# A Mamba and mixture-of-experts block on one core: front products re-spaced between the scans, and constant products added to TensorE

## The reference

```python
h = layernorm(x) * gamma + beta
u, z = split(h @ in_proj.T)                      # 256 channels each
uc = silu(causal_conv4(u) + conv_b)
dt, Bm, Cm = split(uc @ x_proj.T)                # 64, 16, 16
delta = softplus(dt @ dt_proj.T + dt_b)          # 256 channels
state = exp(delta * A) * state + delta * Bm * uc # 256 x 16 states, over 2048 steps
y = (sum_n(state * Cm) + uc * D) * silu(z)
x = layernorm(x + (y @ out_proj.T + x))
probs, experts = top_k(softmax(x @ Wg + bg), 2)  # 8 experts, 128 -> 512 -> 128, gelu
x = layernorm(x + sum_k(probs_k * expert_k(x)))
```

## Time and profile before

| | us |
|---|---|
| three timed runs | 889.17, 895.06, 895.17 |
| median | 895.06 |
| profiled execution, its own time | 891.96 |
| its span | 890.2 |
| first scan to last scan (eight units) | 56.3 to 639.9 |
| mean granted clock of TensorE | 0.764 |

### The profile page before, as it was taken

One profiled execution on the slowest core, in us unless ns is written; L12 is line 12 of the kernel. 1 busy time (PEld: TensorE's weight loads), 2 busy tenths in 40 slices (PEclk: granted clock), 3 DMA queues, 4 the chain that ended last, 5 costly groups with the idle time before them and its releaser, 6 DMA issues. The chain is left out here.

```text
span 890.2 us, 12242 instructions
## 1 busy us (share of the span) xinstructions
PE 678.5 (76%) x2905; PEld 311.1 (35%) x2905; DVE 687.3 (77%) x1350; ACT 423.3 (48%) x884; POOL 530.7 (60%) x526
## 2 busy tenths in 40 slices
PE   3768989878778988878888976878631998899920
PEld 2322222222222322222232221212221888888820
DVE  2167788989998897899889899999732677777754
ACT  3537458357465534735655453324110555455424
POOL 5124546745687757677676677867863455455433
PEclk9885867877987776787797666556555899999975
DMA  3074455565376855547465465655003666666646
GB/s 82 0 202 106 95 127 133 121 152 131 82 189 172 196 135 134 122 115 172 105 142 124 112 142 118 161 120 123 24 27 91 166 177 170 176 168 178 181 128 175
DMA packets 60390, 117.37 MB, mean 132 GB/s; under 512 B 8817, under 2 KB 37297, under 8 KB 52257
## 3 DMA queue, kind: packets, MB, share of 16 engines
q1 hardware_dynamic: 56000, 107.60, 49.4%
q0 software_dynamic: 4320, 8.99, 3.1%
HBM read 100.21 MB, written 16.35 MB: 131 GB/s over the span
## 5 line engine op out<-in xcount | busy, mean ns | idle before, releaser
L532 POOL TENSOR_TENSOR hc<-hs,Crep 128x1024 f32<-128x1024 f32 x128 | 300.1, 2355 | 188.2 <-PE bank L759 102.0
L1295 DVE TENSOR_TENSOR_SCAN hs<-bank,state,flow 128x512 f32<-128x512 f32 x256 | 314.6, 1268 | 58.5 <-ACT bank L1061 53.2
L1061 ACT ACTIVATE bank<-bank,negA 128x512 f32<-128x512 f32 x256 | 165.1, 662 | 253.4 <-PE bank L749 242.0
L749 PE MATMUL bank<-delta,sel 32*128 32x512 f32 x512 | 195.0, 839 | 83.3 <-DVE hs L1295 83.2
L1285 DVE TENSOR_TENSOR flow<-flow,bank 128x2048 f32<-128x2048 f32 x63 | 142.7, 2265 | 0.0
L749 PEld LDWEIGHTS bank<-delta,sel 32*128 32x128 f32 x512 | 50.8, 237 | 212.8 <-DVE hs L1295 145.4
L1189 ACT ACTIVATE flow<-bank,b1T 128x128 f32<-128x128 f32 x284 | 81.1, 369 | 79.8 <-PE bank L926 77.6
L759 PE MATMUL bank<-hc,kc 128*32 128x512 f32 x512 | 91.2, 795 | 6.1 <-POOL hc L532 6.1
L698 PE MATMUL bank<-hT,wtapT 128*128 128x512 f32 x128 | 88.9, 822 | 6.9 <-issue 4.9
L926 PE MATMUL bank<-flow 128*128 128x128 f32 x568 | 83.0, 291 | 14.0 <-issue 9.1
L641 POOL DMA_INDIRECT results<-flow,idn x71 | 69.9, 984 | 33.2 <-issue 31.4
(11 more groups left out here) (180 smaller groups left out, 774.8 us busy)
## 6 DMA issues: line engine op xcount, KB each, us to landing
flow<-du_d SPq DMA_DIRECT2D x63, 1024.0 KB, 7.1
flow<-L_ffn_W SPq DMA_DIRECT2D x71, 256.0 KB
xg<-xs SPq DMA_DIRECT2D x71, 66.0 KB
hs<-results SPq DMA_DIRECT2D x16, 256.0 KB, 4.8
du_d<-du SPq DMA_DIRECT2D x28, 128.0 KB, 3.1
xin<-L_attn_x SPq DMA_DIRECT2D x8, 256.0 KB, 3.1
out<-hc SPq DMA_DIRECT2D x8, 256.0 KB, 2.5
results<-flow,idn POOLq DMA_INDIRECT x71
```

The lines of the kernel that those rows point to most:

```text
L532: nc.gpsimd.tensor_tensor(hc[:, Q % 2, two, :], hs[:, Q % 2, two, :], Crep[u % 3][:].unsqueeze(1).broadcast_to([P, 2, T]), ALU.mult).then_ ...
L749: ins = nc.tensor.matmul(dbank[i][:], sel[32 * i:32 * i + 32, q % 4, :], delta[u % 2][32 * i:32 * i + 32, q // 4, :])
L1061: nc.scalar.activation(dbank[G % 4][:], dbank[G % 4][:], ACT.Exp, scale=negA[:, ch:ch + 1]).then_inc(s_ex, 1)
L1295: nc.vector.tensor_tensor_scan(hs[:, Q % 2, j, :], dbank[G % 4][:], flow[Q % 3][:, j, :], state[:, Q // QUADS % 2, Q % QUADS, j:j + 1], AL ...
```

## The change

TensorE's front work moves by up to two intervals, `spread_b` from g 29 to g 31 behind everything else of the unit; ScalarE's evacuations move with it. In units 1 to 5, at ten places in the order, `keep_busy` adds products of two constant tiles of ones (bf16, 512 columns, 44 a unit) into the front bank that comes next, after a wait until that bank has been drained. GpSimd sets the new tile `idle_rhs` once. Results are not changed: the next user of the bank overwrites it.

```diff
+KEPT_BUSY = {3: (5, "c", 1), 7: (4, "u0", 2), 11: (2, "u0", 2), 13: (2, "u0", 2), 15: (2, "out", -1), 19: (6, "u1", 2),
+             21: (4, "z0", 2), 23: (8, "z1", 2), 25: (5, "xn", -1), 27: (6, "logits", -1)}
...
+            link(nc.gpsimd.memset(idle_rhs[:], 1.0))
...
+            def keep_busy(newest, times):
+                drained(pe, newest - 1)
+                for _ in range(times):
+                    nc.tensor.matmul(fbank[(newest + 1) % 2][:], ones[:], idle_rhs[:])
...
-                    if g == 29 and late:
-                        spread_b(j + 1)
...
                     if late:
+                        if g == 0:
+                            proj_dt(j + 1, 0)
                         if g == 1:
-                            proj_dt(j + 1, 0)
+                            proj_dt(j + 1, 1)
                         if g == 2:
-                            proj_dt(j + 1, 1)
-                        if g == 4:
                             spread_c(j + 1)
...
+                    if late and g == 31:
+                        spread_b(j + 1)
+                    if early and g in KEPT_BUSY:
+                        times, what, ahead = KEPT_BUSY[g]
+                        keep_busy(fill_of(j + ahead, what), times)
```

More of the change, by code:

```diff
@@ L104, in mamba_moe @@
         ones = sb("ones", [P, P], BF16)
+        idle_rhs = sb("idle_rhs", [P, T], BF16)
         w2_sb = sb("w2_sb", [P, E, HK, D])
@@ L817, in host @@
                         first_host(g)
+                        if g == 31:
+                            spread_b(1)
                         continue
                     if late:
+                        if g == 0:
+                            proj_dt(j + 1, 0)
                         if g == 1:
-                            proj_dt(j + 1, 0)
+                            proj_dt(j + 1, 1)
                         if g == 2:
-                            proj_dt(j + 1, 1)
-                        if g == 4:
                             spread_c(j + 1)
-                    if g == 5 and j >= 2:
+                    if g == 4 and j >= 2:
                         ranks(j - 2)
                     if early:
-                        if g == 6:
+                        if g == 5:
                             xhat_T(j + 2)
-                        if g in (8, 9, 10, 12):
-                            conv_u(j + 2, 0, ((8, 9, 10, 12).index(g),))
+                        if g in (7, 8, 10, 11):
+                            conv_u(j + 2, 0, ((7, 8, 10, 11).index(g),))
                     if g == 13:
@@ L836, in host @@
                         out_proj(j - 1, (0, 1))
-                    if g == 16:
+                    if g == 15:
                         out_proj(j - 1, (2, 3))
                     if early:
-                        if g in (17, 18, 20, 21):
-                            conv_u(j + 2, 1, ((17, 18, 20, 21).index(g),))
+                        if g == 16:
+                            conv_u(j + 2, 1, (0,))
+                        if g == 18:
+                            conv_u(j + 2, 1, (1,))
+                        if g == 19:
+                            conv_u(j + 2, 1, (2, 3))
+                        if g == 20:
+                            proj_z(j + 2, 0)
                         if g == 22:
-                            proj_z(j + 2, 0)
-                        if g == 24:
                             proj_z(j + 2, 1)
-                    if g == 25:
+                    if g == 24:
                         xn_T(j - 1)
-                    if g == 28:
+                    if g == 27:
                         logits(j - 1)
@@ L1103, in host @@
                         if g == 4:
+                            c_evac(j + 1)
                             exponential(j + 1)
@@ L1106, in host @@
                             one_plus(j + 1)
-                        if g == 6:
-                            c_evac(j + 1)
                         if g == 8:
@@ L1113, in host @@
                             xhats(j + 2)
-                        if g == 6:
+                        if g == 5:
                             h_evac(j + 2)
-                        if g == 13:
+                        if g == 12:
                             u_evac(j + 2, 0)
+                        if g == 20:
+                            u_evac(j + 2, 1)
                         if g == 21:
-                            u_evac(j + 2, 1)
-                        if g == 22:
                             z_evac(j + 2, 0)
-                        if g == 24:
+                        if g == 23:
                             z_evac(j + 2, 1)
```

## The result

The changed kernel is slower: 906.99 us median of four runs (900.9 to 909.78) against 893.64 (889.17 to 895.17) on the same chip, a ratio of 1.0146 [1.0104, 1.0187] (in brackets, here and below, the 95% interval). Of all the runs of this document two, both of "Tap 0 back", were in a slower state; its median holds them, its ratio doesn't. Its profiled execution took 909.78 us, 17.8 more than that of before (891.96), and its span is 908.0 us. The loop over the units took 598.9 us (57.2 to 656.1) in place of 583.6 (56.3 to 639.9), so 15.3 of the 17.8 us arose there.

The account below looks back on a forecast made before the run. VectorE was taken as the bound, with 53.2 us of scans' waits for ScalarE's exponential as the whole prize; 9.9 us from units 1 to 5 plus 4.5 from units 0 and 6, off 891.96, gave 877.5 us (range 860 to 896).

Parts of the forecast that it names:

- Part 4: Start of units 1 to 5, summed: stalls of 4.3 + 0.4 + 0.7 = 5.4 us left in each, 9.9 us won.
- P: Start of pair 4, counted from scan 0's start: 4.35 us fast, 7.2 us if the clock falls before `spread_c`.
- rival B: Slower, chance 0.12: clock falls at g 2, doesn't recover on fills; 16.9 us lost, 4.5 won, 904.4 us.
- Part 1: Unit's end: `spread_b` to g 31 saves 3.17 us in unit 3, 4.5 us in units 0 and 6 together.
- Part 2: Front work an interval earlier: `spread_c` starts 1.0 us after scan 0 starts, `add_states` done at 3.1.
- Part 3: Price of a fill: 0.25 us fast, 0.45 slow; only the five at g 3 on the path, 1.25 or 2.25.
- Part 4's first half: Unit's start up to scan 6: pair 4 at 7.2 us, a stall of 4.3 us before scans 4 to 6.
- The clock: One fall per unit in place of three, none at softplus or Silu; units 1 to 5 at about 0.85.
- rival C: No change, chance 0.14: fills at g 4 to g 9 eat `spread_b`'s gain; 891.4 us (884 to 899).
- the two things named as what would make the forecast wrong: GpSimd late with hc, so scans wait for L532; or ScalarE's early evacuations waiting for TensorE; no size given.

Follow-up runs that it names:

- Tap 0 back: The changed kernel with the first convolution tap of each unit put back from g 7 to g 8: 891.27 us, ratio 0.9919.
- One-hots early: The changed kernel with the next unit's one-hots moved from behind scan 0 to behind scan 30 of the unit before: 926.46 us, ratio 1.0335.
- GpSimd waits for the one-hots: "Tap 0 back" with GpSimd's last product by C in units 1 to 6 held until the one-hots are done: 881.02 us, ratio 0.9896.
- the best layout: The kernel before with `spread_b` at g 31 ahead of `add_states`, GpSimd's wait for the one-hots and `logits` at g 27, no fills: 864.22 us, ratio 0.9658.
- Only `spread_b`: The kernel before with `spread_b` alone moved from g 29 to g 31, behind `proj_x` and `add_states`: 892.07 us, ratio 0.9938.

## Why the prediction was wrong, point by point

**The step that failed** is in Part 4: "Tap 0 waits for hT, four fills and pair 8 follow", with 0.4 us before scan 9. Tap 0 at g 7 takes the front bank that the ranks filled, and so waits for the run update behind scan 6 too. The change's order on TensorE shows the wait, a second semaphore beside that of ScalarE (line L702):

```
L702 MATMUL bank<-hT,wtapT 128x512 [waits front_bank_drained_by_act,front_bank_drained_by_dve]
```

VectorE frees the bank at 304.42 in unit 3, when scan 6 is done; hT had been there since 302.27. The tap ran at the slow level (2.07 us) with the fills behind it (1.91), so the pair of g 8 came 6.5 us after its release. Forecast for scans 8 and 9 were 2.0 us in five units; the trace shows 24.4 (0.4 of it in unit 6). Moving the tap back gives 1.0146 → 0.9919, and the tap alone costs 1.27% in the kernel before. Both directions were run, so it is shown that the tap's place ahead of the pair made the loss.

The wait is only a part of what came late there. By the forecast's own terms the pair of g 8 starts at P + 8.15 (12.5 in rival B's account, at P = 4.35). With P = 7.8 it started at P + 11.8, 3.7 us later. The tap itself started at P + 8.1, 2.2 us behind hT, which had been forecast as what it waits for (without the run update it would still have stood behind `add_states` until 302.87, 1.6 us earlier than it started). The rest is the level: tap and fills took 3.7 us, where about 2.1 had been counted. So Part 4 also had it wrong that the clock, once back, stays: it came back for 3.4 us and fell again ahead of the tap. In units 2 to 5 the tap started within 0.1 us of the run update's end; unit 1 has no ranks, and there it waited for hT. No run separates the wait from the slow tap and fills.

**A term that was missing**: VectorE's own operations. I priced the one-hots at 0.4 us of VectorE's time, as they were, and never asked what GpSimd does beside them once the scans before them stop waiting. VectorE was busy 9.3 us longer in the loop: one-hots 9.4 us more, the addition of the softplus parts (L1258, median 1966 ns, before 1197) 4.3 more, and others less. It can't simply be added to the waits: in units 3 to 5 it stands in place of the wait for the late pair of g 4. With the tap back its cure gave nothing that could be told; that it is no second cause of the loss in the changed kernel itself is argued from there, since the one run on that kernel ("One-hots early") only moved the collision. In the kernel with `spread_b` at g 31 alone it decides 1.3%.

**Part 1** was right about the place and too hopeful about the price. 19.9 us before scan 30 went to none. But "`add_states` and a product fit" holds only while the scans wait; in the run of `spread_b` alone the inflows waited 8.6 us for it. Ahead of `add_states`, with GpSimd held back and `logits` an interval earlier, it brings 3.4%. The waits of units 0 and 6 fell by 3.5 us of the 4.5, but unit 6 itself didn't become shorter (70.1 us for 69.8): its one-hots collided too, and VectorE was busy 1.1 us longer.

**Part 2** held: `spread_c` waited for the Relu of dt0 and started at +1.7 (+1.0 forecast), `add_states` and the fills behind it.

**Part 3** held in the price: at the slow level the five fills of g 3 take 2.31 us in the timeline above; at the fast level the five of g 25 take

```profile
346.07 1.24 PE L799 MATMUL bank<-idle_rhs,ones 128*128 128x512 bf16 x5
```

A single record lasts 0.38 us (`376/379/379` for the least, median and longest of those fills) and overlaps the next, so start to start is (1.24 - 0.38) / 4 = 0.215 us, and twice that at the slow level; 0.25 and 0.45 had been taken. The Trainium skill ("TensorE: Matmul & The Clock Gate", section "Back-to-back issue gap") gives by its formula for the warm clock 0.216 us for 512 columns, and 0.131 us as what a sustained stream reaches. The trace agrees with the first and not with the second. What failed is "they hide where VectorE's interval is long". Three pairs of kernels say they don't: 1.0146 and 1.0039, 0.9919 and 0.9848, 0.9779 and 0.9658. The one with fills is slower by 0.7 to 1.2% each time; of the second pair the intervals just touch. Nor do "only the five at g 3" lie on the path: the four at g 7, which Part 4 itself sets ahead of the pair of g 8, took 1.9 us there.

**Part 4's first half** held: P = 7.8 us in unit 3 (7.2), and with the collision out of the way scans 4, 5 and 6 wait 2.23 + 0.73 + 1.13 = 4.1 us in unit 3 of the experiment (4.3 forecast). Scan 27 kept 0.7 in four units and 1.1 in unit 5.

**The clock** went as forecast at the softplus work and at Silu. One fall became two: it rose on the five fills at 296.80, fell at 300.20, ahead of the tap, and came back at 317.30. The mean of units 1 to 5 (0.86, 0.82, 0.83, 0.84, 0.91) is the 0.85 named.

**Rival B** had the sign, and with 904.4 us nearly the time, by a road that is half right. Its slow tap (1.9 us) and four slow fills (1.8) are in the trace as 1.87 and 1.84, from start to start. It lacks the wait for the run update and the collisions, and its clock doesn't recover on the fills, where in the trace it did for 3.4 us. That its time comes so near is luck. The range stops at 896 though the prediction lets rival C run to 899; neither holds the 906.99.

**The account of the loop**: forecast 14.4 us won, measured 15.3 lost, a gap of 29.7. Waits of scans were 57.8 us, forecast 38.8: 19.0. VectorE busier: 9.3. Waits of inflows for `spread_b`: 1.7. Together 30.0. Without the 9.3 the scans would probably have waited about as much more: in "GpSimd waits for the one-hots" they waited 9.5 us more for 10.7 us less of one-hots. Neither of the two things named as what would make the forecast wrong came: no scan waited for GpSimd's product, and none for an evacuation that wasn't behind a late pair.

**What stays open.** Why 17 fills at places with slack cost 1.1% in the best layout: idle before scan 7 rose from 4.1 to 9.3 us and before scan 9 from 5.7 to 8.1, and the clock's falls lie elsewhere, but no run separates a fill that delays a pair from one that shifts a fall. The collision of the softplus addition wasn't tried alone. And what the wait for the run update costs by itself isn't known, as said above.

## What to carry to other kernels

Ahead of moving an instruction earlier in the order of an in-order engine, list every semaphore that it waits for at its new place, the one that frees its buffer too, and ask when that comes: all that is queued behind it inherits the wait. One tap moved by one interval cost 1.3% alone, where it was held by hT and the product ahead of it, and 2.3% where it was held by the run update too. And when a stall goes, look beside which operation of another engine the next ones now land: two losses in a row can cover each other, so a cure can read as nothing (0.9919 to 0.9896) in one layout and as 1.3% in another.

Work that is added for the clock's sake must be judged by the time alone. With the tap back, 220 fills raised the granted clock of units 1 to 5 from 0.74 to 0.90, and the five units took 4.8 us longer.

## What the runs showed of the hardware

A product on VectorE of 128x64 elements with both inputs in SBUF took 2.91 us beside a product of GpSimd of 128x1024 that had started 0.47 us after it, and 0.20 us without; GpSimd's took its usual 2.35. The Trainium skill ("SBUF — State Buffer", section "Who interferes with whom") states that a VectorE instruction with two SBUF inputs contends with a GpSimd instruction that reads SBUF; the trace agrees. The page of the Trainium skill also says that issue order decides who blocks. The recorded starts don't show that. In the changed kernel six of the eight one-hots collided, and VectorE's was the one held each time, until about 0.1 us behind the end of GpSimd's. In four of the six VectorE's recorded start was the first, by 0.09 to 0.47 us (289.73 and 290.20 in unit 3), in two GpSimd's. Yet a one-hot that started 0.10 us ahead of GpSimd's product in "Only `spread_b`" (629.71 and 629.81) took 0.20 us. So recorded starts don't tell which instruction had the port first, and no run settles who blocks.
